# Last stage of an audio tower: GpSimd's product v·beta moved behind the norm, and the router's logits in one vector instruction

## The chip, the core and the metric

The kernel runs on one core of a Trainium2 chip, all in fp32. The metric is the device time in microseconds of one execution. A core has five engines with queues of their own that meet only through semaphores: TensorE (PE in the profile, with its weight loads as PEld), VectorE (DVE), ScalarE (ACT), GpSimd (POOL) and SyncE (SP), which here only starts transfers. The last stage, which the change touches, runs from about 1,050 us to the end.

## What is computed

For each of 32 sequences of 750 frames with 256 channels, three residual blocks are computed. The first (self-attention over every second frame, which leaves 384 tokens) and the long parts of the second are done in earlier stages. The last stage finishes the second block, a gated delta rule mixed with two convolutions, and does the third, a mixture of six experts:

```
v = v * beta[..., None];  T = inv(eye + A);  u = T @ v;  w = T @ kb
step(S, q, k, u, w): u2 = u - w @ S; o = q @ S + tril(q @ k.T) @ u2; S = S + k.T @ u2
w = softmax(gelu([x, stats(fir_short, fir_long, delta, v)] @ W1 + b1) @ W2 / temp)
o = w0*fir_short + w1*fir_long + w2*delta + w3*v
h = h + (o * rsqrt(mean(o*o) + 1e-5) * o_norm_w) @ Wo
y = layernorm(h);  q = tanh(y @ proj.T / 0.3)
logits = -((6 - q @ anchors.T) * 0.5) / max(temp_r, 0.1)
weights = softmax over the two largest logits, scattered to the six experts
out = h + sum_e weights[e] * (gelu(y @ w1[e]) @ w2[e])
```

## The kernel before

The last stage takes the sequences one after the other, each as 3 blocks of 128 tokens by 4 heads (12 pairs of block and head). It is a software pipeline of four steps: one **turn** of the code (`body(n, it, e, f)`, written out for each engine) works on the delta rule of sequence n, on gate and mixture of n-1, on output projection, norm, routing and experts 0 to 2 of n-2, and on experts 3 to 5 of n-3. The first four turns and the last three are written out; the 28 between them run in a loop with two turns to a pass, so that every second boundary between turns lies within the loop body and every second one is where the loop goes round. Nothing is scheduled by a program: each engine works through its own queue in the order in which its `body` is written, and stops at each wait until the semaphore has its value. In the loop these values depend on the pass, so register instructions (REGISTER_ALU, ISA in the listings) work them out between the others, and some of these carry a wait themselves.

What the change and the prediction touch:

- **VB = v·beta**, 128x768, made by GpSimd at the start of its turn (L1919) from the packed tile `qa` once the values of before have been read (`r_copied`) and the transfer has landed. PE reads it as the moving operand of `updates(n, o, 0)` (L1313), and DVE subtracts from it in `remainder` (L1676, tile R), which PE waits for in turn (`updates(n, o, 1)`, L1313).
- **GpSimd's other work in a turn**: br = (variance + eps)^-0.5 for the norm (L1924), ta = WT·fir_short (L1927), tb = WT·v (L1929) for the mixture, and r12 = (mean square)^-0.5 (L1933). VB of the next turn follows directly on this last power.
- **DVE**: after that power `normed_mixture` scales the mixture, DL = DL·r12 (L1750, 128x768), and signals `on_ready`, for which `transpose_mixture` on PE waits (L1370). In the middle of its turn DVE runs `second_norm` (y, three instructions, L1775), then waits for the gate's last product (L1711); later comes `routing_logits` (L1780 to L1805), a series of small instructions each of which waits for the one before it, and directly behind it `remainder(n, 1)`.
- **PE** waits for `vb_ready` ahead of the third pair of products (L1245), far ahead of the first use of VB. `transpose_stats` (L1338) waits for the last masked product, which ACT copies (`kk_copied`, L1537); after it `merge_a` (L1255) also waits for `tdiag_ready`.

Of the kernel before, what the change touches and what calls it, by code (L numbers as in the profile page):

```python
# [6 lines left out]
ALU = mybir.AluOpType  # L7
# [971 lines left out]
def third_phase(nc, w, out, shared, tail):  # L979

    NB, dram, bank, ident, upper = (shared[k] for k in ("NB", "dram", "bank", "ident", "upper"))
    with ExitStack() as c:
# [113 lines left out]
        route_step = signal("route_step", 9)  # L1096
# [26 lines left out]
        with nc.Block() as block:  # L1123
# [25 lines left out]
            def _(dve):  # L1149
# [8 lines left out]
                dve.tensor_scalar(bv[:, 0:1], rclip[:, :], 0.1, None, ALU.max).then_inc(setup, 1)  # L1158
# [19 lines left out]
        with nc.Block() as block:  # L1178
# [54 lines left out]
            def _(pe):  # L1233
# [16 lines left out]
                def merge_a(n):  # L1250
                    pe.wait_ge(loaded, 1)
                    pe.wait_ge(*tdiag_ready.now(n))
                    for m in range(NM):
                        for f in (0, 2 * SC):
                            mm = pe.matmul(bank[f // DH][f + SC:f + 2 * SC, m * SC:(m + 1) * SC],  # L1255
                                           ATM[f:f + SC, m, P + f + SC:P + f + 2 * SC], TL[f:f + SC, m, 0:SC],
                                           start=True, stop=True, skip_group_check=True)
                    mm.then_inc(p1_ready.sem, 1)
# [46 lines left out]
                def updates(n, s, b):  # L1305
                    if b == 0:
                        pe.wait_ge(*u12b_copied.now(n))
                        pe.wait_ge(*w_copied.before(n))
                    else:
                        pe.wait_ge(*s_copied.now(n, b))  # L1310
                        pe.wait_ge(*r_copied.now(n, b))
                    for h in range(NH):
                        mm = pe.matmul(bank[2][:, h * DH:(h + 1) * DH], UF[s][:, even_heads_first(b, h), :],  # L1313
                                       R[:, h, :] if b else VB[:, h, :], start=True, stop=True)
                    mm.then_inc(w_ready.sem, 1)
# [104 lines left out]
                def body(n=None, it=None, e=None, f=None, s=0, npair=None, ipair=None):  # L1420
# [18 lines left out]
                    if have_n:  # L1439
                        pe.wait_ge(*vb_ready.now(n))  # L1440
                        products(n, o, 2)
                    if have_f:
                        hidden(f, s, 5)
                    if have_n:
                        pe.wait_ge(*kk_copied.now(n))
                    if have_it:
                        transpose_stats(it)
# [201 lines left out]
            def _(dve):  # L1649
# [128 lines left out]
                def routing_logits(e):  # L1778
# [6 lines left out]
                    dve.tensor_scalar(beats[:, :, :], lg[:, :, :], -float(ND), 0.5, ALU.add, ALU.mult).then_inc(route_step.sem, 1)  # L1785
                    dve.wait_ge(*route_step.now(e, 3))
                    dve.tensor_scalar(lg[:, :, :], beats[:, :, :], rclip[:, 0:1], None, ALU.mult).then_inc(route_step.sem, 1)

                    dve.wait_ge(*route_step.now(e, 4))
# [5 lines left out]
                    dve.wait_ge(*route_step.now(e, 5))  # L1795
# [3 lines left out]
                        .then_inc(lr_ready.sem, 1)  # L1799
                    dve.wait_ge(*route_step.now(e, 6))  # L1800
                    dve.tensor_tensor(cmp[:, :, :, :], cmp[:, :, :, :], eqs[:, :, :, :], ALU.add).then_inc(route_step.sem, 1)
                    dve.wait_ge(*route_step.now(e, 7))
                    dve.tensor_reduce(beats[:, :, :], cmp[:, :, :, :], AX.X, ALU.add).then_inc(route_step.sem, 1)
                    dve.wait_ge(*route_step.now(e, 8))
                    dve.tensor_scalar(lg[:, :, :], beats[:, :, :], 1.5, None, ALU.is_lt).then_inc(route_step.sem, 1)  # L1805

                def routing_weights(e, s):
                    dve.wait_ge(*er_ready.now(e))
                    dve.wait_ge(*route_step.now(e, 9))
# [103 lines left out]
            def _(pool):  # L1913
                def body(n=None, it=None, e=None, s=0, npair=None):
                    o = 1 - s
                    if n is not None:
                        pool.wait_ge(*pa_loaded[o].now(npair))
# [4 lines left out]
                    if e is not None:  # L1922
                        pool.wait_ge(*veps_ready.now(e))
                        pool.tensor_tensor(br[:, :], bv[:, :], minus_half[:, 0:BLK], ALU.pow).then_inc(rstd_ready.sem, 1)  # L1924
# [47 lines left out]
```

## Time and profile before

| | |
|---|---|
| time, median of 3 runs (lowest to highest) | 2969.82 us (2969.29 to 2973.83) |
| the profiled execution: its own time, its span | 2961.62 us, 2959.9 us |
| busy in the span: PE, DVE, ACT, POOL | 2589.0, 1948.2, 1371.9, 531.2 us |
| mean granted TensorE clock | 0.872 |

The busy times are sums over the whole span, which has three stages with different limits. For a change in one stage it matters which engine the others wait for at each point of that stage; the chain that ended last tells it. The granted clock is a share of 2.4 GHz; it has two levels, 1.2 and 2.4 GHz, so a mean of 0.872 says that part of the time was spent at 1.2 GHz.

### The profile page before, as it was taken

Reading aid. Unit: us, or ns where it says so; the run is one execution under the profiler, and the core shown is the slowest. Engines: PE = TensorE matmul, PEld = TensorE weight load, DVE = VectorE, ACT = ScalarE, POOL = GpSimd, SP = SyncE. Lnnn points to the kernel's source line nnn. Section 1 sums busy time; section 2 is a strip of 40 time slices with the busy share of each in tenths; the row PEclk is TensorE's granted clock in tenths of the full one; section 3 lists DMA queues with packets and bytes.
Section 4 is the critical chain, followed back from the end, with each engine's and each line's share of the span. In section 5 each row is a group of like instructions: output and inputs, shape, how many; then the busy total and the mean of one; then the engine's idle time right before and its main releaser. Section 6 shows DMA issues by size and latency. Waiting matters only on the chain.

```text
span 2959.9 us, 60248 instructions
## 1 busy us (share of the span) xinstructions
PE 2589.0 (87%) x21024; PEld 1966.2 (66%) x21024; DVE 1948.2 (66%) x5272; ACT 1371.9 (46%) x2626; POOL 531.2 (18%) x375
## 2 busy tenths in 40 slices
PE   5888888888699279999999999999999999999997
PEld 3666666666588167677667766776776677767765
DVE  4889888888598125656655665566566656655664
ACT  3777777777222023443444434434434444344342
POOL 1334333334100001111111111111111111111110
PEclk8999999999555557998998999899999999999898
DMA  2666666665566702112111211221131113112200
GB/s 72 206 206 201 200 212 197 212 202 192 198 238 221 207 22 97 63 62 101 61 63 63 101 59 63 68 97 63 57 105 61 63 63 103 61 60 66 97 17 16
DMA packets 233222, 334.12 MB, mean 113 GB/s; under 512 B 113696, under 2 KB 198656, under 8 KB 223776
## 3 DMA queue, kind: packets, MB, share of 16 engines
q1 hardware_dynamic: 207168, 305.89, 31.4%
q10 hardware_dynamic: 24672, 12.58, 1.4%
q0 software_dynamic: 1152, 12.58, 1.1%
q8 instruction: 144, 2.36, 0.3%
q14 instruction: 86, 0.70, 0.1%
HBM read 191.68 MB, written 164.23 MB: 120 GB/s over the span
## 4 chain that ended last, share of the span: by engine, by line
PE 43%; DVE 11%; ACT 5%; issue 5%; DVEq 0%; ACTq 0%
PE bank L1407 6%; PE bank L1417 6%; PE bank L1350 5%; PE bank L1328 3%; PE bank L1361 3%; PE bank L1379 3%; PE bank L1313 3%; PE bank L1245 2%; PE bank L1354 2%; ACT L1554 2%; PE bank L1277 2%; PE bank L1285 2%; DVE HA L1826 1%; DVE bst L1762 1%; PE bank L1370 1%
## 5 line engine op out<-in xcount | busy, mean ns | idle before, releaser
L1417 PE MATMUL bank<-w2e,HE 128*128 128x256 f32 x1152 | 318.6, 417 | 12.5 <-DVE HA L1826 9.6
L1407 PE MATMUL bank<-YT,w1e 128*128 128x384 f32 x768 | 325.9, 552 | 1.3 <-ACT HE L1554 1.3
L683 DVE SCALAR_TENSOR_TENSOR Y<-bank,convw,Y 128x383 f32<-128x383 f32 (+2 forms) x576 | 315.4, 608 | 7.1 <-ACT Y L559 7.1
L1826 DVE SCALAR_TENSOR_TENSOR HA<-bank,we,HA 128x256 f32<-128x256 f32 x576 | 242.7, 477 | 108.0 <-PE bank L1417 105.8
L411 PE MATMUL bank<-pb,wqkv 128*128 128x384 f32 x768 | 288.1, 506 | 10.4 <-DVE pb L667 9.5
L1711 DVE TENSOR_TENSOR L<-bank,b2g 128x48 f32<-128x48 f32 x32 | 6.7, 208 | 412.5 <-PE bank L1361 412.5
L1417 PEld LDWEIGHTS bank<-w2e,HE 128*128 128x128 f32 x1152 | 224.8, 207 | 55.3 <-issue 16.9
L1927 POOL TENSOR_TENSOR ta<-qb,WT 128x768 f32<-128x768 f32 x32 | 72.5, 2266 | 741.5 <-DVE WT L1730 741.5
L1407 PEld LDWEIGHTS bank<-YT,w1e 128*128 128x128 f32 x768 | 153.0, 217 | 77.0 <-issue 30.4
L1350 PE MATMUL bank<-qb,w1g 128*128 128x384 f32 x512 | 201.8, 517 | 0.4 <-ACT GH L1546 0.4
L1537 ACT ACTIVATE ATM<-bank 128x192 f32<-128x192 f32 x192 | 60.2, 331 | 302.2 <-DVE ATM L1653 302.2
L1245 PE MATMUL bank<-qa 64*128 64x256 f32 x768 | 120.6, 436 | 90.8 <-PEq L1123 58.0
L1554 ACT ACTIVATE HE<-bank 128x384 f32<-128x384 f32 x192 | 94.3, 491 | 223.4 <-PE bank L1407 222.1
L411 PEld LDWEIGHTS bank<-pb,wqkv 128*128 128x128 f32 x768 | 138.9, 198 | 84.8 <-issue 15.6
L783 POOL TENSOR_TENSOR RR<-RS,minus_half 128x24 f32<-128x24 f32 x32 | 133.3, 4164 | 272.7 <-DVE RS L732 272.7
L1245 PEld LDWEIGHTS bank<-qa 64*128 64x128 f32 x768 | 72.6, 202 | 137.2 <-issue 120.1
L559 ACT ACTIVATE Y<-bank,convw 128x384 f32<-128x384 f32 x192 | 112.2, 585 | 81.2 <-PE bank L411 80.1
L909 PE MATMUL bank<-v_all,toep 128*128 x512 | 129.5, 434 | 20.5 <-DMA toep<-toeplitz 18.4
L1933 POOL TENSOR_TENSOR m<-m,minus_half_q 128x12 f32<-128x12 f32 x32 | 72.6, 2268 | 400.4 <-DVE m L1746 400.4
L1328 PEld LDWEIGHTS bank<-W,ATM 128*128 128x128 f32 x768 | 118.5, 231 | 30.6 <-ACT W L1529 19.7
L1328 PE MATMUL bank<-W,ATM 128*128 128x64 f32 x768 | 124.8, 316 | 10.0 <-ACT W L1529 10.0
L909 PEld LDWEIGHTS bank<-v_all,toep 128*128 128x128 f32 x512 | 114.0, 328 | 28.2 <-issue 21.5
(221 smaller groups left out, 5512.6 us busy)
## 6 DMA issues: line engine op xcount, KB each, us to landing
packa<-pa SPq DMA_DIRECT2D x32, 1932.0 KB, 6.3
qa<-packa SPq DMA_DIRECT2D x32, 1932.0 KB, 7.7
packb<-pb SPq DMA_DIRECT2D x32, 768.0 KB, 5.1
qb<-packb SPq DMA_DIRECT2D x32, 768.0 KB, 6.4
toeplitz<-taps SPq DMA_DIRECT2D x128, 190.0 KB, 4.3
toep<-toeplitz SPq DMA_DIRECT2D x32, 760.0 KB, 4.3
packb<-fsk SPq DMA_DIRECT2D x32, 384.0 KB, 2.3
fl<-fl SPq DMA_DIRECT2D x32, 384.0 KB, 5.0
```

Source lines behind the costliest of these rows:

```text
L411: mm = pe.matmul(proj_bank[j][:, 0:T], wqkv[:, a, j * P:(j + 1) * P], xnT[:, a, :], start=(a == 0), stop=(a == HALF - 1))
L559: act.activation(Y[:, j, :], proj_bank[j][:, 0:T], ACT.Copy, scale=convw[:, j, CK - 1:CK])\
L683: dve.scalar_tensor_tensor(out=Y[:, j, lag:T], in0=proj_bank[j][:, 0:T - lag], scalar=convw[:, j, CK - 1 - lag:CK - lag], in1=Y[:, j, lag: ...
L783: pool.tensor_tensor(RR[:, :, :, :].rearrange("p b n h -> p (b n h)"), RS[:, :], minus_half[:, :], ALU.pow)\
L909: pe.matmul(acc[:, o:o + BLK * NB], toep[s][:, ch, 0:P], v_all[:, it * CG + ch, :], start=(k == 0), stop=False, skip_group_check=True)
L1245: mm = pe.matmul(bank[odd][:, hh * 2 * P:(hh + 1) * 2 * P], kT[rows, hh, pair * P:(pair + 1) * P], qkb[rows, :, hh, pair * P:(pair + 1) * ...
L1328: mm = pe.matmul(bank[1][:, h * DH:(h + 1) * DH], ATM[:, even_heads_first(b, h), 0:P], W[:, h, :], start=(b == 0 and h == 0), stop=True, s ...
L1350: pe.matmul(mlp_bank[m][:, 0:T], w1g[:, a, m * P:(m + 1) * P], chans(pb[s], PX)[:, a, :], start=(a == 0), stop=False)
L1407: mm = pe.matmul(bank[6][:, 0:T], w1e[:, a, k, :], YT[s][:, a, :], start=(a == 0), stop=(a == HALF - 1))
L1417: mm = pe.matmul(expert_bank(b), HE[k % 2][:, b * P:(b + 1) * P], w2e[:, k, :], start=True, stop=True)
L1554: act.activation(HE[k % 2][:, :], bank[6][:, 0:T], ACT.Gelu_apprx_tanh).then_inc(he_ready.sem, 1)
L1826: dve.scalar_tensor_tensor(out=HA[s][:, b, :], in0=expert_bank(b), scalar=we[s][:, b, k:k + 1], in1=HA[s][:, b, :], op0=ALU.mult, op1=ALU. ...
```

## The change

On GpSimd, the power for the norm comes first in a turn, and VB behind it, once all three `y` instructions of DVE have signalled. On PE the wait for `vb_ready` moves from the third pair of products to just ahead of `updates(n, o, 0)`, and the wait for `tdiag_ready` from `merge_a` to just ahead of `transpose_stats`. On DVE the logits, before (lg - 6)·0.5 and then ·rclip, become one instruction (lg - 6)·rclip with rclip spread over the 18 columns as a second tensor; rclip holds half of its old value, which the setup sees to. The later waits of that series, renumbered by one, are not shown.

```diff
@@ setup of the last stage, DVE
-                dve.tensor_scalar(bv[:, 0:1], rclip[:, :], 0.1, None, ALU.max).then_inc(setup, 1)
+                dve.tensor_scalar(bv[:, 0:1], rclip[:, :], 0.1, 2.0, ALU.max, ALU.mult).then_inc(setup, 1)
@@ PE
                 def merge_a(n):
                     pe.wait_ge(loaded, 1)
-                    pe.wait_ge(*tdiag_ready.now(n))
...
                 def updates(n, s, b):
                     if b == 0:
+                        pe.wait_ge(*vb_ready.now(n))
                         pe.wait_ge(*u12b_copied.now(n))
...
                     if have_n:
-                        pe.wait_ge(*vb_ready.now(n))
                         products(n, o, 2)
                     if have_f:
                         hidden(f, s, 5)
                     if have_n:
                         pe.wait_ge(*kk_copied.now(n))
+                        pe.wait_ge(*tdiag_ready.now(n))
@@ DVE, routing_logits
-                    dve.tensor_scalar(beats[:, :, :], lg[:, :, :], -float(ND), 0.5, ALU.add, ALU.mult).then_inc(route_step.sem, 1)
+                    dve.scalar_tensor_tensor(out=lg[:, :, :].rearrange("p b e -> p (b e)"), in0=lg[:, :, :].rearrange("p b e -> p (b e)"),
+                                             scalar=-float(ND), in1=rclip[:, 0:1].broadcast_to([P, BLK * NE]),
+                                             op0=ALU.add, op1=ALU.mult).then_inc(route_step.sem, 1)
+
                     dve.wait_ge(*route_step.now(e, 3))
-                    dve.tensor_scalar(lg[:, :, :], beats[:, :, :], rclip[:, 0:1], None, ALU.mult).then_inc(route_step.sem, 1)
-
-                    dve.wait_ge(*route_step.now(e, 4))
@@ GpSimd
+                    if e is not None:
+                        pool.wait_ge(*veps_ready.now(e))
+                        pool.tensor_tensor(br[:, :], bv[:, :], minus_half[:, 0:BLK], ALU.pow).then_inc(rstd_ready.sem, 1)
                     if n is not None:
+                        if e is not None:
+                            pool.wait_ge(*y_ready.now(e))
                         pool.wait_ge(*pa_loaded[o].now(npair))
                         pool.wait_ge(*r_copied.before(n))
                         pool.tensor_tensor(VB[:, :, :], heads(pa[o], VTOK),
                                            pa[o][:, VBS:VBS + NM].unsqueeze(2).broadcast_to([P, NM, DH]), ALU.mult)\
                             .then_inc(vb_ready.sem, 1)
-                    if e is not None:
-                        pool.wait_ge(*veps_ready.now(e))
-                        pool.tensor_tensor(br[:, :], bv[:, :], minus_half[:, 0:BLK], ALU.pow).then_inc(rstd_ready.sem, 1)
```

On GpSimd's queue the first turn of the loop body reads as follows before:

```order
L1918 ISA [waits pa_loaded0]
L1919 TENSOR_TENSOR VB<-qa 128x768 [waits r_copied]
L1923 REGISTER_ALU
L1924 TENSOR_TENSOR b<-b,minus_half_q 128x3 [waits q_veps_ready]
L1926 ISA
L1927 TENSOR_TENSOR ta<-qb,WT 128x768 [waits wt_step]
L1929 TENSOR_TENSOR tb<-qa,WT 128x768
L1933 TENSOR_TENSOR m<-m,minus_half_q 128x12 [waits ms_ready]
```

and with the change (`b` is br, `m` is r12):

```order
L1918 TENSOR_TENSOR b<-b,minus_half_q 128x3 [waits q_veps_ready]
L1921 ISA
L1922 ISA [waits y_ready]
L1923 ISA [waits pa_loaded0]
L1924 TENSOR_TENSOR VB<-qa 128x768 [waits r_copied]
L1928 ISA
L1929 TENSOR_TENSOR ta<-qb,WT 128x768 [waits wt_step]
L1931 TENSOR_TENSOR tb<-qa,WT 128x768
L1935 TENSOR_TENSOR m<-m,minus_half_q 128x12 [waits ms_ready]
```

VB stood directly behind the power m of the turn before; now the power b and the wait for y stand between them.

On PE's queue the piece of the loop body around the third pair of products and the transposed statistics changes as follows (qa 128x256 are the products, SG the statistics):

```order
-L1440 REGISTER_ALU
-L1241 REGISTER_ALU [waits vb_ready]
-L1245 MATMUL bank<-qa 128x256 [waits kk_copied]
-L1245 MATMUL bank<-qa 128x256 x3
-L1407 MATMUL bank<-YT,w1e 128x384 [waits he_ready]
-L1407 MATMUL bank<-YT,w1e 128x384
-L1445 REGISTER_ALU
-L1338 MATMUL bank<-ident,SG 32x128 [waits std_ready,h2_ready,mean_ready,kk_copied]
+L1241 REGISTER_ALU
+L1245 MATMUL bank<-qa 128x256 [waits kk_copied]
+L1245 MATMUL bank<-qa 128x256 x3
+L1407 MATMUL bank<-YT,w1e 128x384 [waits he_ready]
+L1407 MATMUL bank<-YT,w1e 128x384
+L1444 REGISTER_ALU
+L1445 REGISTER_ALU [waits kk_copied]
+L1338 MATMUL bank<-ident,SG 32x128 [waits std_ready,h2_ready,mean_ready,tdiag_ready]
```

One register instruction goes ahead of the products; ahead of the transposes, the wait for `kk_copied` has moved from the matmul itself to a register instruction in front of it.

On DVE's queue the routing of a turn in the loop changes as follows:

```order
 L1783 TENSOR_REDUCE e<-c 128x18 [waits route_step]
 L1784 REGISTER_ALU
-L1785 TENSOR_SCALAR e<-e 128x18 [waits route_step]
-L1786 REGISTER_ALU
-L1787 TENSOR_SCALAR e<-e,rclip 128x18 [waits route_step]
+L1785 SCALAR_TENSOR_TENSOR e<-e,rclip 128x18 [waits route_step]
 L1789 REGISTER_ALU
 L1792 TENSOR_TENSOR c<-e 128x108 [waits route_step]
```

Two instructions have become one; what stands ahead of them and behind them is as it was.

## Rows read from the trace of the kernel before

**Rows 1.** Page, part 4: shares on the chain that ended last.
```profile
PE 43%; DVE 11%; ACT 5%; issue 5%; DVEq 0%; ACTq 0%
```

**Rows 2.** The chain, 1990 to 2115 us: start, us, engine, tile, line.
```profile
2033.51 0.96 DVE c L1780
...
2034.79 1.06 DVE e L1785
2035.88 0.25 DVE e L1787
2036.15 0.06 DVE c L1792
...
2037.86 0.41 DVE R L1676
...
2038.41 1.08 PE bank L1313 x8
```

**Rows 3.** Who waited for whom, 1110 to 2960 us: us, times, longest.
```profile
PE bank L1313 <- DVE R L1676: 30.0, 23, 1.4
...
PE bank L1338 <- ACT ATM L1537: 9.2, 30, 2.8
...
PE bank L1370 <- DVE DL L1750: 2.0, 10, 0.2
```

**Rows 4.** The chain between the two turns of the loop body.
```profile
2109.67 2.17 DVE DL L1750
...
2111.89 0.87 PE bank L1370 x6
...
2115.23 1.49 PE bank L1417 x6
```

**Rows 5.** Three DVE lines: count, duration in ns as min/median/max.
```profile
L1780 DVE TENSOR_TENSOR c<-e,anchors x32: 271/948/1564, 1162.3 to 2931.8; 128x108 f32<-128x108 f32 x32
...
L1785 DVE TENSOR_SCALAR e<-e x32: 176/1052/1055, 1162.9 to 2932.4; 128x18 f32<-128x18 f32 x32
...
L1750 DVE TENSOR_TENSOR DL<-DL,m x32: 948/2176/2178, 1124.0 to 2909.8; 128x768 f32<-128x768 f32 x32
```

**Rows 6.** Timeline of GpSimd, 2000 to 2130 us: start, us, instruction.
```profile
2032.06 2.27 POOL L1927 TENSOR_TENSOR ta<-qb,WT 128x768 f32<-128x768 f32 x1 [22.46 <-DVE WT L1730]
2034.29 1.52 POOL L1929 TENSOR_TENSOR tb<-qa,WT 128x768 f32<-128x768 f32 x1
...
2107.32 2.27 POOL L1933 TENSOR_TENSOR m<-m,minus_half_q 128x12 f32<-128x12 f32 x1 [10.92 <-DVE m L1746]
2109.55 1.47 POOL L1919 TENSOR_TENSOR VB<-qa 128x768 f32<-128x768 f32 x1
```

**Rows 7.** Timeline of DVE, 2046 to 2108 us.
```profile
2073.32 1.04 DVE L1775 TENSOR_SCALAR y<-HA,bmv,b 128x256 f32<-128x256 f32 x3
2087.07 0.21 DVE L1711 TENSOR_TENSOR L<-bank,b2g 128x48 f32<-128x48 f32 x1 [12.71 <-PE bank L1361]
```

**Rows 8.** The chain, 1990 to 2115 us.
```profile
2084.19 2.85 PE bank L1361 x24
```

**Rows 9.** The chain where the loop goes round.
```profile
2168.14 2.23 issue
...
2171.50 0.80 PE bank L1370 x6
...
2174.66 1.49 PE bank L1417 x6
```

**Rows 10.** The chain, 2060 to 2080 us.
```profile
2062.46 2.60 PE bank L1379 x12
...
2065.27 0.69 DVE HA L1758
```

**Rows 11.** Windows of two turns: length, busy us by engine, PEclk, DMA.
```profile
1655.69:1776.58 120.89, 113.33 (x823) 85.20 (x822) 70.83 (x211) 49.76 (x90) 16.60 (x11) 0.89 0.21 70
...
2008.75:2123.63 114.88, 106.19 (x823) 79.51 (x822) 73.01 (x211) 49.43 (x90) 16.60 (x10) 0.96 0.22 74
```

More of the change, by code:

```diff
@@ L1095, in third_phase @@
         z_ready, q_ready = signal("z_ready"), signal("q_ready", primed=2)
-        route_step = signal("route_step", 9)
+        route_step = signal("route_step", 8)
         lr_ready, er_ready = signal("q_lr_ready"), signal("er_ready")
@@ L1794, in routing_logits @@
                     dve.tensor_reduce(me[:, :], lg[:, :, :], AX.X, ALU.max).then_inc(route_step.sem, 1)
-                    dve.wait_ge(*route_step.now(e, 5))
+                    dve.wait_ge(*route_step.now(e, 4))
                     dve.tensor_tensor(eqs[:, :, :, :], eqs[:, :, :, :], before_e[:, :, :].unsqueeze(1).broadcast_to([P, BLK, NE, NE]), ALU.mult)\
@@ L1799, in routing_logits @@
                         .then_inc(lr_ready.sem, 1)
+                    dve.wait_ge(*route_step.now(e, 5))
+                    dve.tensor_tensor(cmp[:, :, :, :], cmp[:, :, :, :], eqs[:, :, :, :], ALU.add).then_inc(route_step.sem, 1)
                     dve.wait_ge(*route_step.now(e, 6))
-                    dve.tensor_tensor(cmp[:, :, :, :], cmp[:, :, :, :], eqs[:, :, :, :], ALU.add).then_inc(route_step.sem, 1)
+                    dve.tensor_reduce(beats[:, :, :], cmp[:, :, :, :], AX.X, ALU.add).then_inc(route_step.sem, 1)
                     dve.wait_ge(*route_step.now(e, 7))
-                    dve.tensor_reduce(beats[:, :, :], cmp[:, :, :, :], AX.X, ALU.add).then_inc(route_step.sem, 1)
-                    dve.wait_ge(*route_step.now(e, 8))
                     dve.tensor_scalar(lg[:, :, :], beats[:, :, :], 1.5, None, ALU.is_lt).then_inc(route_step.sem, 1)
@@ L1808, in routing_weights @@
                     dve.wait_ge(*er_ready.now(e))
-                    dve.wait_ge(*route_step.now(e, 9))
+                    dve.wait_ge(*route_step.now(e, 8))
                     dve.tensor_tensor(ex[:, :, :], ex[:, :, :], lg[:, :, :], ALU.mult).then_inc(we_step.sem, 1)
```

## The prediction, made before the changed kernel had run

> **What bounds the kernel now.** I read the shares of the chain first: PE carries 43% of it, DVE 11%, ACT 5% and issue 5% [rows 1]; in the last stage the chain goes from PE to DVE and back in every turn, so an instruction of DVE counts where PE stands still behind it, and nowhere else. Then I followed the chain through two turns. In the middle of a turn it runs along the small instructions of `routing_logits`, through R (L1676) and into PE's L1313 [rows 2], because `remainder` stands behind the routing in DVE's queue; the list of waits shows PE waiting for R 23 times, 30.0 us in all [rows 3]. Two of these lie in the turn of n=1, which has no routing: 21 count. At the end of a turn the chain can run through L1750, for which PE's transposes (L1370) wait 10 times, but only 2.0 us in all [rows 3, 4].
>
> Next I laid GpSimd beside DVE. L1785 has 18 elements and takes 1.05 us in the median, 0.18 us at best; L1780 takes 0.95 us and 0.27 us at best; L1750 takes 2.18 us and 0.95 us at best [rows 5]. Each ends just behind an instruction of GpSimd: L1780 ends at 2034.47 and ta at 2034.33, L1785 at 2035.85 and tb at 2035.81, L1750 at 2111.84 and VB at 2111.02, with some 0.8 us of its own work still to do [rows 2, 4, 6]. So these DVE instructions wait for GpSimd's to end, and do not share with them. The median of L1750 says that at least half of its 32 executions meet VB.
>
> **GpSimd: VB moves behind y.** VB takes 1.47 us wherever it stands [rows 6]. It will start when y is written, at about 2073.32 + 1.04 = 2074.4, and end near 2076. DVE is idle from there until L1711 at 2087.07, 12.7 us later [rows 7], so nothing is there to be blocked. Its first reader, L1313 of `updates(n, o, 0)`, stands behind L1361, which ends at 2084.19 + 2.85 = 2087.04 [rows 8]: 11 us of cover, and PE's moved wait for it costs nothing. If that cover were gone, each of the 30 turns with a VB would pay up to 1.47 us, 44 us in all. On GpSimd's queue the products ta and tb stand behind VB; they wait for WT until about 2092.6 in that turn and are not late. The power b now stands ahead of VB and waits for the variance as before. No transfer is issued by GpSimd, and SP's waits are on signals that do not move.
>
> What the move gives is at L1750: 2.17 us become about 0.95 us. But PE had waited only 0.20 us each time [rows 3]; behind that, its own work binds. From L1370 to L1417 the chain takes 2115.23 - 2111.89 = 3.34 us where PE had waited, and 2174.66 - 2171.50 = 3.16 us where it had not [rows 4, 9]. So a boundary inside the loop body gains 0.20 + 0.18 = 0.38 us, and ten of them 3.8 us. The bounds are 2.0 us (the waits alone) and the same 3.8 us. Where the loop goes round, PE issues nothing for 2.23 us [rows 9] and L1750 is done by then: nothing is gained there. What DVE has late next is the masked product of the next turn, for which PE's own products come first.
>
> **DVE: two instructions become one.** L1785 and L1787 go, and one takes their place. The new one starts where L1785 did, while tb runs. Nothing in the trace is this operation from SBUF alone; it is bounded from both sides. If it waits for tb as L1785 did, it ends where L1785 ended, and L1792 moves up by 2036.15 - 2035.88 = 0.27 us. If it does not, it ends at once, L1792 meets tb instead, and, as L1780 did after ta, ends 0.14 us after tb, at 2035.95 and not at 2036.15 + 0.27 = 2036.42: 0.47 us [rows 2, 6]. I take 0.27 us, since both nearest rows, L1785 with one tensor read and L1780 with two, did wait. On the path it counts 21 times, and twice more in the last two turns, where DVE's chain is bare: 23 x 0.27 = 6.2 us, and 10.8 us at the upper bound. In the other nine turns R waits for PE anyway. The Trainium skill's page "SBUF — State Buffer", section "Who interferes with whom", says that a DVE instruction with two SBUF inputs and a GpSimd instruction that reads SBUF exclude each other for their whole length. By that rule the new instruction, whose rclip is now a tensor, waits for tb: 6.2 us; with a free one the sum would be up to 4.6 us better. The trace agrees so far, with 0.95 against 0.27 us for L1780.
>
> **PE: the waits.** One register instruction less stands ahead of the products, behind a matmul that is still running: nothing. Ahead of L1338 the wait for `kk_copied` moves to a register instruction, and this wait ends last: PE stands still for ACT's copy 30 times there [rows 3]. After such a wait the matmul has still to be issued. The trace has no such wait on PE that ends last. On DVE, L1758 behind a wait of this form starts at 2065.27, 0.21 us after L1379 has ended (2062.46 + 2.60) [rows 10]; L1711, which carries its wait itself, starts 0.03 us after L1361 [rows 7, 8]. The cost lies between 0 and 0.18 us a turn; I take the middle, 0.09 us, since DVE's case carries more waits in its row. It falls on all 28 turns of the loop, since what follows L1338 (ACT's copy, the experts' gelu, the copy P for which PE waits) is on the chain as well: 28 x 0.09 = 2.5 us, at most 5.0 us. The wait for `tdiag_ready` itself is long over, since DVE writes TL before the last masks.
>
> **Sum.** 3.8 + 6.2 - 2.5 = 7.5 us less. Against the profiled execution's own time, 2961.62 us (span 2959.9 us), that is 2954.1 us. The median of the three runs shown stands 8.2 us higher, at 2969.82 us; from it, **2962.3 us**. The terms' bounds give a gain of 2.0 + 6.2 - 5.0 = 3.2 us at the least and of 3.8 + 10.8 - 0 = 14.6 us at the most. About 0.2%, 5.9 us, is what a measurement of this kernel can tell from no change.
>
> **Rivals.**
>
> The gain is too small to be seen. The register instruction costs its full 0.18 us and the boundary gains only the 0.20 us waited: 3.2 us, 2966.6 us. For it speaks that PE's waits are short (0.20 us at L1370), and that the 2.18 us of L1750 are mostly hidden; against it that PE waits 1.3 us on average for R, so that 0.27 us less there can't be lost on another engine.
>
> The clock gives more back. In two windows of the same two turns the granted clock was 0.89 and 0.96 on average, and the length 120.89 and 114.88 us: 0.86 us for each hundredth [rows 11]. If less idle time of PE lifts the clock by one hundredth through some 15 such pairs of turns, 13 us come on top: about 2949 us. The windows do not show what decides which of them gets the lower level, and the same code gets both. The Trainium skill's "TensorE: Matmul & The Clock Gate", "What's actually happening", has the clock throttled unless activity releases it, which would let a kernel with fewer gaps run more at 2.4 GHz; the two windows bear out only that the level varies.
>
> Slower: the wait in front of L1338. It has to cost more than (3.8 + 6.2) / 28 = 0.36 us a turn to take all of the gain, and (10.0 + 5.9) / 28 = 0.57 us to be seen as slower; at 0.6 us the kernel would take 2969.8 + 6.8 = 2976.6 us. Against it stands the 0.21 us of L1758, the largest such gap in these rows; for it only that PE's pipeline behind a register instruction has not been seen waiting.
>
> **Chances.** The forecast case, a gain from 5.9 to 14.6 us: 0.48. The clock case: 0.12. Too small to be seen: 0.34. Slower: 0.06. So faster 0.60, same 0.34, slower 0.06. The range goes from 2951 us (the upper bound of the sum, 2955.2 us, and part of the clock case) to 2970 us (no gain at all).
>
> **What the new profile would show.** L1750 at 0.95 us in every turn and no wait of L1370 for it; VB between y and L1711; the new routing instruction at 1.05 us, with L1792 directly behind it (at 0.18 us instead, L1792 would be the long one); PE's wait for R shorter by 0.27 us; L1338 starting 0.04 us after ACT's copy if the register instruction is free, 0.1 to 0.2 us after it if not. I would be wrong if VB met another DVE instruction in its new place, if L1750 met the power or something else of GpSimd's, or if the time of a pair of turns at the same granted clock did not fall by about 0.5 us.

## The result, and the profile after

The changed kernel takes 2937.96 us (median of five executions, 2935.36 to 2952.54), the kernel before 2969.82 us beside it. The ratio of the means is 0.9898, with a 95% interval of [0.9873, 0.9924]. That is faster, as forecast, but by 1.07% in the medians and not by 0.25%, and it lies below the range. The profiled execution took 2936.39 us, its span is 2934.7 us and its mean granted clock 0.888, where it was 0.872 before.

The single steps first. For each of the two DVE lines that the change is about, the profile gives the count and the duration (min/median/max, ns):

```profile
L1750 DVE TENSOR_TENSOR DL<-DL,m x32: 947/948/959, 1123.8 to 2888.4; 128x768 f32<-128x768 f32 x32
...
L1785 DVE SCALAR_TENSOR_TENSOR e<-e,rclip x32: 177/1054/1058, 1162.4 to 2908.6; 128x18 f32<-128x18 f32 x32
```

L1750 never meets VB now (2.18 us in the median before, [rows 5]); the new routing instruction takes 1.05 us. GpSimd's timeline of one turn shows VB behind the wait for y, long done when it is read:

```profile
2052.39 0.85 POOL L1918 TENSOR_TENSOR b<-b,minus_half_q 128x3 f32<-128x3 f32 x1 [17.65 <-DVE b L1770]
2058.92 1.47 POOL L1924 TENSOR_TENSOR VB<-qa 128x768 f32<-128x768 f32 x1 [5.68 <-DVE y L1775]
2075.98 2.27 POOL L1929 TENSOR_TENSOR ta<-qb,WT 128x768 f32<-128x768 f32 x1 [15.59 <-DVE WT L1730]
```

The chain through the routing (start, us, what) answers to [rows 2]:

```profile
2020.80 1.06 DVE e L1785
2021.86 0.02 issue
2021.88 0.06 DVE c L1792
...
2023.60 0.13 DVE R L1676
```

From the start of L1785 to R it takes 2.80 us, 0.27 us less than the 2037.86 - 2034.79 = 3.07 us of before. The list of waits, 1110 to 2940 us (us, times, longest), answers to [rows 3]:

```profile
PE bank L1313 <- DVE R L1676: 24.2, 23, 1.2
PE bank L1338 <- ACT ATM L1537: 22.1, 29, 2.8
...
DVE bmv L1767 <- DVE bst L1762: 6.5, 14, 0.5
PE bank L1370 <- DVE DL L1750: 0.5, 1, 0.5
```

The longest wait for R fell from 1.4 to 1.2 us. But PE now stands still 22.1 us ahead of L1338, not 9.2, and DVE has a wait that was not in its list before. Both lie on the chain of the changed kernel, here in the first turn of a pass:

```profile
2050.25 1.09 DVE bst L1762 x3
2051.39 0.41 issue
2051.80 0.33 DVE bmv L1767 x3
...
2053.03 0.34 ACT ATM L1537
2053.37 0.33 issue
2053.70 0.50 PE bank L1338 x3
```

The same place in the kernel before:

```profile
2066.32 1.09 DVE bst L1762 x3
...
2067.50 0.32 DVE bmv L1767 x3
...
2068.74 0.34 ACT ATM L1537
2069.08 0.04 issue
2069.12 0.52 PE bank L1338 x3
```

Behind ACT's copy PE needs 0.33 us and not 0.04, so 0.29 us more in each of 28 turns; the gap ahead of bmv is 0.41 us where it was 2067.50 - (2066.32 + 1.09) = 0.09 us, in 14 turns. Together these two cost 8.1 + 4.5 us, which accounts for the 22.1 - 9.2 = 12.9 us that PE's wait ahead of L1338 grew by, and so eat what R and L1750 give. The 30 us came from elsewhere. Windows over the last stage (length, busy us of PE, PEld, DVE, ACT, POOL, mean PEclk, DMA share, GB/s), of before:

```profile
1110.00:2915.00 1805.00, 1683.26 (x12508) 1266.22 (x12507) 1108.13 (x3224) 760.24 (x1377) 258.62 (x156) 0.92 0.21 70
```

and after:

```profile
1110.00:2915.00 1805.00, 1667.05 (x12581) 1250.44 (x12579) 1088.03 (x3232) 766.91 (x1390) 260.24 (x157) 0.94 0.21 71
```

In 1805 us, 0.02 more of the clock is an estimated 70 us less at 1.2 GHz. Read from the clock's own record in the two traces, from 1110 us to the end, it is 304 us before and 217 us after, 87 us less.

**What a hundredth of the clock is worth.** Each execution has a time and a mean granted clock. Within one and the same kernel they go together: four executions of e18 below took 2957.13, 2953.94, 2936.32 and 2920.80 us at a clock of 0.877, 0.883, 0.888 and 0.897. (Its two others, 2973.24 and 2970.24 us at 0.872 and 0.873, lie over 1.5% above its fastest, count as slow, and are left out of its ratio and its row below.) A line through 196 executions of the 20 kernels, with a level of its own for each kernel, falls by 20 us for each 0.01 of the clock (standard error 0.8). So a difference between kernels can be split: what goes with the clock, and what is left when both are put at the same clock, the **direct** part. The table has both, with the standard error of the direct part at a slope of exactly 20 us (the slope's own error adds up to 1.3 us for a kernel as far off in clock as the changed one, 2.4 us for e6); the **stall** is PE's idle time ahead of the first L1313 that waits for R, in the last stage, median of those over 0.7 us. "Wide" and "narrow" are an added 512-column and 16-column matmul; before is all its 73 executions; the ratio is that of the means. The changed kernel is 1.6 us slower than before at the same clock, which can't be told from no difference, and 32.0 us faster by its clock.

| kernel | ratio to before [95%] | mean clock | direct, us | stall, us |
|---|---|---|---|---|
| before | 1 | 0.8706 | 0 | 1.43 |
| changed | 0.9898 [0.9873, 0.9924] | 0.8866 | +1.6 ± 1.0 | 1.15 |
| e1 VB and PE's waits | 1.0075 [1.0055, 1.0096] | 0.8634 | +7.0 ± 1.2 | 1.43 |
| e2 logits alone | 0.9907 [0.9882, 0.9932] | 0.8843 | -3.7 ± 2.2 | 1.16 |
| e3 changed, cheap wait | 0.9886 [0.9862, 0.9910] | 0.8857 | -6.9 ± 1.2 | 1.15 |
| e4 PE's waits alone | 1.0068 [1.0047, 1.0088] | 0.8648 | +6.8 ± 1.0 | 1.43 |
| e5 VB, cheap wait | 0.9977 [0.9960, 0.9993] | 0.8718 | -3.3 ± 0.8 | 1.42 |
| e6 six matmuls | 0.9921 [0.9899, 0.9943] | 0.9005 | +37.2 ± 1.4 | none |
| e7 longer routing | 1.0031 [1.0013, 1.0050] | 0.8686 | +4.3 ± 1.0 | 1.57 |
| e8 e3, R early | 0.9874 [0.9849, 0.9899] | 0.8858 | -7.0 ± 1.3 | none |
| e9 before, wide | 0.9893 [0.9864, 0.9922] | 0.8880 | +5.3 ± 1.9 | none |
| e10 e3, wide | 0.9891 [0.9869, 0.9914] | 0.8852 | -2.7 ± 1.6 | none |
| e11 before, narrow | 0.9897 [0.9882, 0.9911] | 0.8855 | -0.5 ± 1.3 | 1.29 |
| e12 e2, wide | 0.9861 [0.9838, 0.9884] | 0.8902 | +0.9 ± 1.6 | none |
| e13 before, narrow, ahead | 0.9847 [0.9825, 0.9869] | 0.8935 | -2.4 ± 2.4 | 1.20 |
| e14 e2, narrow | 0.9881 [0.9861, 0.9901] | 0.8845 | -7.6 ± 1.0 | 1.03 |
| e15 e7, narrow | 1.0019 [0.9995, 1.0043] | 0.8690 | +2.9 ± 1.2 | 1.44 |
| e16 e1, narrow | 0.9922 [0.9906, 0.9938] | 0.8830 | +1.9 ± 1.6 | 1.30 |
| e17 e2, longer | 0.9917 [0.9898, 0.9936] | 0.8818 | -3.8 ± 1.3 | 1.37 |
| e18 e15, two narrow | 0.9895 [0.9855, 0.9935] | 0.8863 | +2.9 ± 2.0 | 1.22 |

### The profile page after: what moved, and what is told of

Its sections match the earlier page's. It is cut to its first block, busy times and chain, and to the rows that moved or that the text cites. A ratio compares the mean times of both kernels' runs of the same rounds, so it can differ in the third digit from the quotient of the medians.

```text
span 2934.7 us, 60213 instructions
## 1 busy us (share of the span) xinstructions
PE 2552.5 (87%) x21024; PEld 1936.5 (66%) x21024; DVE 1916.4 (65%) x5240; ACT 1371.2 (47%) x2626; POOL 532.7 (18%) x375
## 4 chain that ended last, share of the span: by engine, by line
PE 42%; DVE 11%; ACT 6%; issue 6%; DVEq 0%; ACTq 0%; POOL 0%
PE bank L1407 6%; PE bank L1417 6%; PE bank L1350 5%; PE bank L1361 3%; PE bank L1379 3%; PE bank L1245 3%; PE bank L1328 3%; ACT L1554 3%; PE bank L1354 2%; PE bank L1313 2%; PE bank L1276 2%; PE bank L1284 2%; DVE DL L1740 1%; DVE HA L1826 1%; DVE bst L1762 1%
## 5 line engine op out<-in xcount | busy, mean ns | idle before, releaser
L1407 PE MATMUL bank<-YT,w1e 128*128 128x384 f32 x768 | 321.1, 545 | 1.2 <-ACT HE L1554 1.2
L1417 PE MATMUL bank<-w2e,HE 128*128 128x256 f32 x1152 | 308.9, 407 | 10.8 <-DVE HA L1826 7.8
L1407 PEld LDWEIGHTS bank<-YT,w1e 128*128 128x128 f32 x768 | 150.5, 214 | 75.5 <-issue 27.8
L1328 PEld LDWEIGHTS bank<-W,ATM 128*128 128x128 f32 x768 | 108.0, 212 | 35.8 <-ACT W L1529 25.7
L1328 PE MATMUL bank<-W,ATM 128*128 128x64 f32 x768 | 114.5, 298 | 15.0 <-ACT W L1529 15.0
```

Of the source, the lines that this page charges most:

```text
L1328: mm = pe.matmul(bank[1][:, h * DH:(h + 1) * DH], ATM[:, even_heads_first(b, h), 0:P], W[:, h, :], start=(b == 0 and h == 0), stop=True, s ...
L1407: mm = pe.matmul(bank[6][:, 0:T], w1e[:, a, k, :], YT[s][:, a, :], start=(a == 0), stop=(a == HALF - 1))
L1417: mm = pe.matmul(expert_bank(b), HE[k % 2][:, b * P:(b + 1) * P], w2e[:, k, :], start=True, stop=True)
```

## The experiments: which part of the change does it

**e1: VB moved and PE's waits as in the changed kernel, old logits.**

```diff
@@ the changed kernel, DVE
-  one scalar_tensor_tensor
+  the two tensor_scalar of before
```

> VB moved with PE's waits as in the changed kernel, the logits in two instructions as before. Direct terms as the two profiles now show them: L1750 loses 1.2 us but PE had waited only ten times (3.8 us gained), and PE starts L1338 about 0.33 us later after ACT's copy in each of 28 turns (about 8 us lost). If only such terms count, the kernel is 4 to 5 us slower than before, 2974 us. If the gain of the changed kernel comes through the granted clock, and the clock follows from how GpSimd and DVE stand to each other at the end of a turn, it is about 20 us faster, 2950 us, with a mean clock near 0.884; if the clock follows from the shorter routing, it stays near 0.872.

Measured: 2992.70 us, slower than before. Two thirds of the change by itself lose 0.75%, so the gain stands or falls with the logits.

**e2: the logits alone.**

```diff
@@ the kernel before, DVE
-  the two tensor_scalar
+  one scalar_tensor_tensor
```

> Before, with the logits in one instruction and nothing else. Direct term: 0.27 us in 23 turns, 6.2 us less, 2963.6 us, with the clock as before (0.872). If the clock follows from the routing (R, for which PE waits, is 0.27 us earlier), more: 20 us faster or better, with a mean clock of 0.88 or above.

Measured: 2941.33 us, 0.9907 of the time before. One small instruction less gives nearly the whole gain on its own, of which only 3.7 us are direct.

**e3: the changed kernel with its two waits ahead of L1338 in the other order, so that the one for `kk_copied` sits on the matmul.**

```diff
@@ the changed kernel, PE
                     if have_n:
+                        pe.wait_ge(*tdiag_ready.now(n))
                         pe.wait_ge(*kk_copied.now(n))
-                        pe.wait_ge(*tdiag_ready.now(n))
```

> The changed kernel with two waits of PE in the other order, so that the one that ends last (for the copied product) is carried by the matmul L1338 itself and the register instruction ahead of it carries the one for TL. If the register instruction costs what the new profile shows, L1338 starts 0.04 us after ACT's copy and not 0.33 to 0.38 us, 28 times: 8 to 9 us faster than the changed kernel, 2929 us. If the chain absorbs it, within 2 us of the changed kernel. If the clock is what counts, the sign is open: less idle time should not lower the clock, so 2920 to 2932 us.

Measured: 2932.97 us, and PE's wait there is

```profile
PE bank L1338 <- ACT ATM L1537: 14.0, 29, 2.8
```

8.1 us less than in the changed kernel, as its chain says; the direct part fell by 8.5 us. This version beats both kernels in the median, though its interval meets that of the changed one.

**e4: only PE's waits moved.**

```diff
@@ the kernel before, PE: updates(n, o, 0); products(n, o, 2); ahead of transpose_stats; merge_a
+                        pe.wait_ge(*vb_ready.now(n))
...
-                        pe.wait_ge(*vb_ready.now(n))
...
                         pe.wait_ge(*kk_copied.now(n))
+                        pe.wait_ge(*tdiag_ready.now(n))
...
-                    pe.wait_ge(*tdiag_ready.now(n))
```

> Before, with PE's two waits where the changed kernel has them, VB and the logits as before. By the direct term 28 x 0.3 us = 8 to 9 us slower than before, 2978 us, at an unchanged clock. If the clock reacts to any shift of PE's work and not to idle time, the time can go either way by 10 us or more with a mean clock that moves by 0.005 or more.

Measured: 2988.31 us. The direct loss is 6.8 us, 0.24 us a turn; another 11.6 us go with a lower clock, 0.8648.

**e5: VB moved, waits as in e3, old logits.**

```diff
@@ e3, DVE
-  one scalar_tensor_tensor
+  the two tensor_scalar of before
```

> VB behind y and PE's wait for VB where the changed kernel has it, but PE's last wait before L1338 carried by the matmul, and the logits in two instructions. With the register instruction's cost gone, only what the move of VB does is left. If the first term of the prediction holds (ten boundaries, 0.38 us each): 3.8 us faster than before, 2963.6 us. If the move is worth nothing, 2967 us. If the loss of the VB kernel of the first four (2992.7 against 2967.4 us) is the register wait's doing and not the move's, the loss of 25 us is gone here.

Measured: 2963.96 us, direct -3.3 us: VB's term, where 3.8 us were forecast. Its clock, 0.8718, is nearly that of the kernel before, 0.8706.

## The experiments: what moves the clock

In the kernel before, a stretch of PE's timeline (idle before it in brackets):

```profile
2212.74 1.08 PE L1313 MATMUL bank<-R,UF 128*128 128x64 f32 x8 [1.43 <-DVE R L1676]
2213.65 0.66 PE L1302 MATMUL bank<-S,qa 128*128 128x128 f32 x4
2214.29 1.97 PE L1328 MATMUL bank<-W,ATM 128*128 128x64 f32 x8
2216.05 2.87 PE L1407 MATMUL bank<-YT,w1e 128*128 128x384 f32 x4
2218.71 1.06 PE L1321 MATMUL bank<-W,qa 128*128 128x128 f32 x4
```

and the windows over it:

```profile
2211.00:2213.00 2.00, 0.57 (x5) 0.29 (x3) 1.87 (x9) 0.61 (x2) 0.00 (x0) 1.00 0.91 240
...
2214.00:2216.00 2.00, 2.00 (x11) 1.84 (x11) 1.90 (x6) 0.24 (x1) 0.00 (x0) 0.55 0.98 417
2216.00:2218.00 2.00, 2.00 (x5) 1.17 (x5) 1.44 (x4) 0.00 (x0) 0.00 (x0) 0.50 0.99 366
```

PE stands still for R, and 1.5 us after it starts again the granted clock is 0.50, that is 1.2 GHz, though it is fully busy: the last column but two of these rows is the clock. L1328, L1407 and L1321 take 1.97, 2.87 and 1.06 us there. The same groups in the changed kernel, where the clock stayed full behind a shorter stall:

```profile
2024.14 1.08 PE L1313 MATMUL bank<-R,UF 128*128 128x64 f32 x8 [1.16 <-DVE R L1676]
...
2025.69 1.10 PE L1328 MATMUL bank<-W,ATM 128*128 128x64 f32 x8
2026.63 1.51 PE L1407 MATMUL bank<-YT,w1e 128*128 128x384 f32 x4
2027.98 0.61 PE L1321 MATMUL bank<-W,qa 128*128 128x128 f32 x4
```

with the window

```profile
2026.00:2028.00 2.00, 2.00 (x13) 1.47 (x12) 1.90 (x8) 0.00 (x0) 0.00 (x0) 1.00 0.98 417
```

The first thought was that PE has too little to do around this stall, the next that the length of the stall counts.

**e6: six 128-column matmuls whose result nobody reads, in the stall.**

```diff
@@ the kernel before, PE, body
+                    if have_e and have_n:
+                        for _ in range(6):
+                            pe.matmul(bank[2][:, 0:P], ident[:, :], upper[:, 0:P], start=True, stop=True)
                     if have_n:
                         updates(n, o, 1)
```

> Before, with six extra 128x128 matmuls on PE (about 0.9 us, results never read, in columns that the next matmuls overwrite) just ahead of the matmuls that wait for R, in every turn that routes and has a next sequence. Nothing on DVE, ACT or GpSimd is different. If the granted clock answers to how busy PE is there, fewer stretches at 1.2 GHz: mean clock from 0.872 to 0.885 or more, and 2935 to 2950 us, although work was added. If the gain of the one-instruction logits came from R being earlier in itself and not from PE's idle time, nothing is won and the eight or nine turns in which PE is not waiting pay 0.9 us each: 2975 us, clock at 0.872.

Measured: 2947.13 us at the highest clock of all, 0.9005: by the clock alone it would gain 60 us. It pays 37.2 us directly; most of it is PE having nothing issued ahead of the products, now twice in a pass and not once:

```profile
PE bank L1245 <- issue: 58.1, 26, 2.6
```

In the kernel before this was 26.4 us in 13 times.

**e7: R later, by one more small instruction of DVE onto a spare tile.**

```diff
@@ the kernel before, DVE, routing_logits
+                    dve.tensor_scalar(spare[:, :, :], beats[:, :, :], rclip[:, 0:1], None, ALU.mult)
                     dve.tensor_scalar(lg[:, :, :], beats[:, :, :], rclip[:, 0:1], None, ALU.mult).then_inc(route_step.sem, 1)
```

> Before, with one more small instruction of DVE (18 elements, about 0.2 us, onto a spare tile) in the routing, so that R and what PE does behind it come later. By the direct term about 0.2 us in 23 turns, 5 us slower: 2972 us. If the granted clock answers to PE's idle time in front of R, the loss is several times that: 2985 us or more at a mean clock under 0.868. If the gain of the one-instruction logits was a matter of luck with the phase of the clock, the time may go either way.

Measured: 2979.40 us, stall 1.57 us, direct +4.3 ± 1.0 us; PE waits for R 26 times there, and 26 x 0.14 = 3.6 us. The clock hardly moves. Making the stall longer costs little, making it shorter (e2) gives much.

**e8: e3 with R made in the middle of the routing, so that PE hardly waits for it.**

```diff
@@ e3, DVE
-                        routing_logits(e)
+                        routing_logits(e, (lambda: remainder(n, 1)) if have_n else None)
@@ routing_logits, behind the maximum me
+                    if between is not None:
+                        between()
```

> The changed kernel with the cheap order of waits, and DVE makes R in the middle of the routing (behind the instruction that finds the largest logit) instead of behind all of it. R comes about 1.1 us earlier where PE waited for it 1.0 to 1.2 us. By the direct term 20 turns x 1.1 us = 22 us less than the 2933 us of the kernel it is made from: 2911 us. If the clock gives as much again: 2890 to 2905 us, mean clock 0.895 or more. Against it: in turns where R waits for PE, the tail of the routing now stands behind that wait, and the mixture's next products on DVE are up to 1.3 us later; if that binds, 2933 us or more.

Measured: 2933.31 us, no more than e3 (2932.97). The wait has only moved on, to the state:

```profile
PE bank L1293 <- DVE S L1687: 46.5, 31, 1.7
```

which was 22.1 us in e3.

**e9, e10, e12: one 512-column matmul in the stall, in the kernel before, e3 and e2. e11: the same with 16 columns in the kernel before, as control.**

```diff
@@ PE, body
+                    if have_e and have_n:
+                        pe.matmul(bank[2][:, 0:512], ident[:, :], w1s[:, 0:512], start=True, stop=True)
                     if have_n:
                         updates(n, o, 1)
@@ e11
+                        pe.matmul(bank[2][:, 0:16], ident[:, :], w1s[:, 0:16], start=True, stop=True)
```

> Before, with a single extra matmul of 512 columns ahead of the matmuls that wait for R (about 0.86 us, result never read). The kernel with six small ones gained 24 us although it got a second idle stretch of about 2.3 us behind each passage of the loop's end, 30 us in all, which I put down to the twelve added instructions. If one instruction does not bring that second stretch and the clock answers to PE's idle time in front of R, this gives both: 2915 to 2930 us, mean clock 0.895 or more. If the clock theory is wrong, 2971 to 2978 us at 0.872.

> The same matmul in the changed kernel with the cheap order of waits (2933 us). There PE's idle time in front of R is already shorter, and part of the clock's gain is taken. If idle time in front of R is what lowers the clock, the rest goes too: 2905 to 2920 us, mean clock 0.90 or more. If the one-instruction logits gained in another way, the two add up in full: 2885 us. If the changed kernel has nothing left to gain there: 2933 to 2940 us.

> Before with the one-instruction logits and the 512-column matmul, VB where it was. If the first term of the prediction (0.38 us at ten to fourteen boundaries inside the loop body) is right, this is 4 to 5 us slower than the kernel with VB moved as well; if VB's move does nothing, equal to it.

> Control for the kernels with extra matmuls: before, with one extra matmul of 16 columns at the same place. It has the same instructions and the same places of all others in the queue as the one with 512 columns, but next to no work. By the clock theory the same as before, 2967 to 2975 us, mean clock 0.870 to 0.875. If the gain came from where the instructions fall and not from PE's work, it equals the kernel with 512 columns.

Measured: 2944.38, 2936.02, 2931.32 and, with 16 columns, 2939.14 us. The control gains as much as the wide one in the kernel before, so it is not the amount of work. What the narrow one does to PE's timeline:

```profile
2020.41 0.29 PE L1498 MATMUL bank<-w1s,ident 128*128 128x16 f32 x2
2021.99 1.08 PE L1313 MATMUL bank<-R,UF 128*128 128x64 f32 x8 [1.30 <-DVE R L1678]
```

Its stall is 0.13 us shorter than in the kernel before, since the added matmul stands in it.

The expectations from here on set two theories against each other: by A the length of PE's stall for R decides the clock, by B any small change of what PE does in a turn shifts where the low stretches fall.

**e13: the 16-column matmul ahead of `expert_out(e, 0)`, not behind it. e14, e15, e16: as in e11, but in e2, e7 and e1.**

```diff
@@ e13: the kernel before, PE, body
+                    if have_e and have_n:
+                        pe.matmul(bank[2][:, 0:16], ident[:, :], w1s[:, 0:16], start=True, stop=True)
                     if have_e:
                         expert_out(e, 0)
```

> The kernel before with the same 16-column matmul on PE once a turn, but ahead of the three matmuls of expert_out(e, 0) instead of behind them, so that nothing stands still behind it. PE still has its 1.4 us stall for R in full. Theory A, what counts is that the stall for R is broken or shortened (the narrow matmul behind the expert cut it from 1.43 to 1.29 us): no gain, 2966 to 2975 us. Theory B, the two levels of the clock fall differently with any small change of what PE does in a turn: a change of up to 1% either way, most likely another gain, 2935 to 2955 us.

> The one-instruction logits alone, with the 16-column matmul behind expert_out(e, 0). Theory A (length of the stall for R decides): the stall falls from 1.16 to about 1.0 us, and the gain grows beyond that of either alone, to 2925 us or less. Theory B (any small change shifts where the clock's low stretches fall): the two gains, 30 us each, do not add; between 2930 and 2960 us, and it could as well be worse than the logits alone.

> The kernel before with one more small DVE instruction in the routing (which alone made it 0.3% slower, R later by 0.25 us) and the 16-column matmul behind expert_out(e, 0). Theory A: the stall is 1.54 us, longer than in the kernel before, and the kernel takes 2970 to 2980 us. Theory B: no relation to the stall; the direct cost of R is 6 us, and the clock gives anything between a gain of 30 and a loss of 10 us.

> VB moved and PE's waits as in the changed kernel, two-instruction logits (2992.7 us by itself), with the 16-column matmul behind expert_out(e, 0). Theory A: stall for R shortened by 0.13 us as in the kernel before, so the same gain of 30 us: 2960 to 2965 us. Theory B: no prediction of the sign; a result above 2985 us would speak against A.

Measured: 2922.20, 2933.82, 2975.67 and 2946.69 us. By its words theory A failed in e13, the fastest kernel of all: I had taken its stall to be untouched. But the trace has it at 1.20 us, since the expert's matmuls end later:

```profile
2015.55 1.08 PE L1313 MATMUL bank<-R,UF 128*128 128x64 f32 x8 [1.20 <-DVE R L1678]
```

e15 came in the time that A gave, though with a stall of 1.44 us and not 1.54: with the stall back at the length of before, the same matmul gives nothing. e16 gained more than A's 30 us, e14 less than A's. With the stalls side by side, all kernels fall into two groups: 1.42 us and more, clock 0.863 to 0.872; 1.30 us and less, or none, clock 0.883 to 0.9005. Within a group a shorter stall gives no more (e14 has 1.03 us and 0.8845, e2 1.16 us and 0.8843). That was seen only now, so two kernels were set up on it.

**e17: e2 with two small instructions of DVE on spare tiles. e18: e15 with a second 16-column matmul, ahead of the expert.**

```diff
@@ e17: e2, DVE, ahead of the scalar_tensor_tensor
+                    dve.tensor_scalar(spare[:, :, :], lg[:, :, :], rclip[:, 0:1], None, ALU.mult)
+                    dve.tensor_scalar(spare2[:, :, :], lg[:, :, :], rclip[:, 0:1], None, ALU.mult)
@@ e18: e15, PE, body
+                    if have_e and have_n:
+                        pe.matmul(bank[2][:, 0:16], ident[:, :], w1s[:, 0:16], start=True, stop=True)
                     if have_e:
                         expert_out(e, 0)
```

> The one-instruction logits alone (2941 us, stall for R 1.16 us in the median of its stalls over 0.7 us) with two more small DVE instructions in the routing, on spare tiles, which should put R back by some 0.14 us each, to a stall of about 1.43 us as in the kernel before. In the traces so far all six kernels with a stall of 1.42 to 1.57 us spent 311 to 395 us of the last stage at 1.2 GHz, and all ten with 1.30 us or less, or none, 163 to 271 us. Theory A (the length of this stall decides): over 300 us at 1.2 GHz and 2965 to 2985 us, so no gain left though the instructions themselves cost only 6 us. Theory B (any change shifts the levels at will): direct cost alone, 2941 + 6 = 2947 us, give or take 15.

> The longer routing (one more DVE instruction) with a 16-column matmul on both sides of expert_out(e, 0). With one of them behind the expert the stall was 1.44 us and the time 2976 us; the one ahead shortened the stall by 0.23 us in the kernel before, so here about 1.2 us. Theory A: below 275 us at 1.2 GHz, 2935 to 2955 us. Theory B: no reason for a gain over the kernel with one, 2960 to 2985 us. If the stall stays over 1.4 us, nothing is told.

Measured: 2945.96 us for e17, the number of theory B, and with 266 us at 1.2 GHz, where A gave over 300. But its stall came to 1.37 us, between the two groups:

```profile
2029.09 1.07 PE L1314 MATMUL bank<-R,UF 128*128 128x64 f32 x8 [1.37 <-DVE R L1677]
```

So it does not decide. e18, stall 1.22 us, has the median of all six executions at 2955.54 us, at the edge of what A gave, and that of the four in its row at 2945.13 us, within it. But these four go from 2920.80 us (clock 0.897) to 2957.13 us (0.877), so one program with one stall is spread over 0.020 of the clock: the stall does not fix the outcome. Of the means, that of e17, 0.8818 at a stall of 1.37 us, lies between the groups, and none contradicts them.

**What follows each stall.** Theory A can be put to the single stalls. For every stall for R over 0.7 us in the 20 profiled executions, the clock's record tells whether the clock fell to 1.2 GHz within 2.6 us of PE starting again, and how long it stayed there. It was at 2.4 GHz during every one of them. (From 1110 us on; one execution of each kernel.)

| kernel | stalls over 0.7 us | followed by a fall | us at 1.2 GHz begun there | us at 1.2 GHz elsewhere |
|---|---|---|---|---|
| before | 21 | 18 | 130 | 174 |
| changed | 21 | 10 | 34 | 183 |
| e1 | 24 | 24 | 239 | 145 |
| e2 | 19 | 7 | 24 | 192 |
| e7 | 25 | 25 | 184 | 132 |
| e8 | 0 | 0 | 0 | 227 |
| e11 | 20 | 10 | 68 | 164 |
| e13 | 24 | 7 | 31 | 133 |
| e15 | 21 | 21 | 188 | 157 |
| e18 | 14 | 7 | 38 | 234 |

Over all 20, each of the 119 stalls of 1.42 us and more was followed by a fall, and 91 of the 188 shorter ones. The one DVE instruction that e15 has more than e11 makes the difference between 21 of 21 and 10 of 20. From before to changed, the time at 1.2 GHz behind the stalls falls by 96 us and that elsewhere rises by 9. So it is shown where the gain lies: in the low clock behind PE's stall for R. The table also shows where this gain ends. Without any such stall, e8 has 227 us at 1.2 GHz elsewhere, no less than the changed kernel has in all; and the profiled execution of e18 has 38 us behind R and 234 us elsewhere, so its spread need not come from this stall.

## Why the prediction was wrong, point by point

- **GpSimd: VB moves behind y** held: PE and DVE wait for VB nowhere, L1750 is at its best time in every turn, and PE's wait for L1750 is gone but for one. The term of 3.8 us measured 3.3 ± 0.8 us (e5).
- **DVE: two instructions become one** held in its place: the new instruction waits for tb as its neighbours did (1.05 us), and R comes 0.27 us sooner. As the Trainium skill's "SBUF — State Buffer", section "Who interferes with whom", has it, the operation with a second SBUF tensor is excluded by GpSimd's; the trace agrees (177 ns at best, 1,054 in the median), though it does not test the second tensor as the reason: the old L1785, with one, took 1,052 in the median as well. Of the 6.2 us some 4.5 us go back in a gap I had not counted, DVE's 0.32 us more ahead of L1767 in 14 turns. It stands in the trace of every kernel with the one instruction and of no other, except that e17, with two more ahead of it, does not have it either; what makes it is not shown. The measured term is 3.7 ± 2.2 us (e2) or 6.9 - 3.3 = 3.6 us (e3 against e5); the 6.2 - 4.5 = 1.7 us that would be left by these rows lie within the error.
- **PE: the waits** was mis-sized: 0.09 us a turn was forecast, 0.18 us the bound. The chain has 0.29 us, e4 gives 6.8 / 28 = 0.24 us, and the changed kernel against e3 (1.6 + 6.9) / 28 = 0.30 us. The bound was taken from DVE's rows and did not hold on PE. So the sum at equal clock is -3.3 - 3.6 + 8.5 = +1.6 us and not -7.5 us. That it meets the +1.6 us of the changed kernel says nothing, since two of the three are differences to e3; from e5, e2 and e4, each against before, it is -3.3 - 3.7 + 6.8 = -0.2 us. Either way the direct terms alone bring nothing.
- **The step that failed** is the clock: the sum had no term for it, and it stood only as the rival "The clock gives more back", with a chance of 0.12 and 13 us. The mean clock went up by 0.016 and gave 32 us, more than four times the sum of the terms. The price in the rows held: 0.86 us for each hundredth of a pair of turns. What failed is the size of the shift, one hundredth through some 15 pairs. Over the stage the clock rose by 2.3 hundredths (304 us at 1.2 GHz before, 217 after), and 0.86 x 15 x 2.3 = 30 us. I let a hundredth go with less idle time of PE in general; the runs show that the whole difference sits behind one recurring stall, which went from 1.43 to 1.15 us and was then followed by a fall 10 times of 21 and not 18. The length of this stall is not all that counts: in e4 it is unchanged and a wait elsewhere in the turn is longer, and the falls behind it last 205 us and not 130, with a mean clock 0.6 of a hundredth lower. That the time came out faster, as forecast, was luck as far as the terms go: they cancel.
- Of the signs of being wrong that I had named, the last one came: a pair of turns did not get 0.5 us shorter at the same clock, since the direct part is +1.6 us in all.

What stays open is why a stall that is 0.3 us shorter lets the clock stand about every second time, and what sets the low time elsewhere in the stage (132 to 235 us from kernel to kernel). The Trainium skill's "TensorE: Matmul & The Clock Gate", section "What's actually happening", ties the clock to activity, and no run here contradicts that; but 16 columns (e11) brought what 512 did (e9), and e18 was at 0.877 and at 0.897 with one program. Whether a shift in time against something else on the chip has a part in it was not told apart.

## What to carry to other kernels

Where a kernel's granted clock is below 1, compare variants at equal clock as well as in time: fit the time against the clock over all executions, and judge an edit by what is left, since a gain of 1% here had a direct part that can't be told from nothing. Price the clock as a case of its own, with the measured slope, and give it a real chance when the edit touches a stall of TensorE that recurs in every turn; a nearly free matmul in front of such a stall is worth a try (1.5% in e13, but nothing in e15, where the stall stayed at 1.44 us). Look at what the clock does behind each stall, and not only at its mean. Put the wait that ends last on the matmul itself, and those long over on the register instructions ahead of it.

## What the runs showed of the hardware

- A wait that ends last on a register instruction of PE costs 0.24 to 0.30 us against one on the matmul; on DVE the nearest such row had 0.21 us.
- A 16-column fp32 matmul, 0.29 us once a turn, brought 31 us (e11) and, three matmuls further ahead, 45 us (e13), nearly all of it by the clock.
- PE has about 2.1 us with nothing issued where the loop goes round (25 to 29 us in 13 times) in every kernel but e6; with 12 more instructions in the body (e6) there is a second such gap of about the same length.
- Of 119 stalls of TensorE of 1.42 to 1.57 us, all at 2.4 GHz, every one was followed by a fall to 1.2 GHz within 2.6 us of its going on; of 188 of 0.7 to 1.39 us, 91 were (20 traces).
- Four executions of one program, e18, differ by 1.2% in time and by 0.020 in the mean clock.
